# A two-layer kernel on one core: the front's order of work, and the fill of a scatter buffer on another queue

## The chip, the cores and the metric

The kernel runs on 1 core of one Trainium2 chip. The metric is the device time of one execution in microseconds (us), the median of several runs. A core has five engines that work side by side: PE (TensorE, matrix products and transposes), DVE (VectorE), ACT (ScalarE), POOL (GpSimd) and SP (SyncE, which here only issues DMA transfers). They meet through semaphores. SP, ACT and POOL issue transfers, each on its own queue, and all of them are carried by the same 16 DMA engines of the core.

## The reference, cut to what matters

Layer 0 adds to x a selective state-space model (SSM) and a top-1 mixture of 8 experts, both of the layer norm of x. Layer 1 adds attention and a top-4 mixture of 60 experts. There are 2 batches of 1024 tokens, of 256 features each.

```python
xn = _layernorm(x)
x_dbl = einsum('bld,ed->ble', xn, x_proj_w)
dt, B_in, C_in = split(x_dbl, [128, 144])            # 128 step columns, 16 of B, 16 of C
delta = softplus(einsum('blr,dr->bld', dt, dt_proj_w) + dt_proj_b)
dA  = exp(dt_t[..., None] * A[None])                 # per token, feature and one of 16 states
dBx = dt_t[..., None] * B_t[:, None, :] * x_t[..., None]
h = dA * h + dBx
y_t = einsum('bdn,bn->bd', h, C_t) + D_param * x_t
```

## The kernel before

The kernel is written engine by engine; each engine's instructions run in the order written, and that order is set by hand. What the change touches is the front (the first 90 us) and the state loop behind it.

**The front.** `ln(0)` on DVE makes the normalised tokens `xn` in 4 groups of 512 tokens. PE turns each group (L1894), ACT copies it to `xnT` (L1809), PE multiplies it with the step columns (L1904, copied by ACT to `dtT`, L1813) and with the B, C and router columns (L1910, copied by DVE to `bcT`, L1687). `dt_piece(p)` (L1914) projects the step sizes in four pieces: batch p // 2, feature half p % 2. For each piece ACT takes the absolute value, the positive part, an exponential and four squares (L1821 to L1827), and DVE combines them in five steps to `delta` (L1705, L1707); the buffers of a piece are those of `decay`, `state` and `hc`, used in turn by even and odd pieces (L207). PE turns `bcT` (L1926), and DVE copies the B columns `b_col` (L1691) and routes the tokens to the 8 experts (`route_dve`, L420, with a short part on PE, `route_pe`, L477); its `slots_ready` releases 16 indirect DMAs on POOL (`route_pool`, L489), which scatter the tokens to `sorted0`. Before, the routing came on DVE ahead of all four softplus pieces. `delta_rows(b)` (L1932) turns delta back on PE, and DVE multiplies it with `xn` to `dxT` (L1711).

**The fill.** The scatter buffer of layer 1, `sorted1` (124 tiles of 128 rows of 256 numbers, 15.5 MB), has to be zero before it is scattered into. ACT issues this fill behind the softplus pieces, ahead of the state loop: 15 transfers of 1 MB and one of 0.5 MB from a tile of zeros, 128 partitions of 8 KB each (`zero_fill`, L506). Its semaphore `zeroed` is waited for by DVE (L1766) and ACT (L1854) ahead of layer 1.

**The state loop.** 32 iterations `it`, 16 states for each of two batches, and in each two feature halves c. ACT scales `dxT` to `dbxT` (L1842) and makes `decay` (L1848), PE turns `dbxT` into PSUM (`spread`, L1948, its matmuls L1956), DVE scans (L1723), POOL multiplies the scanned state with the C row `crow[:, q]` (L1602, `hc`), and PE sums the products (`gather_sum`, L1959, its matmuls L1962). q is the parity of the iteration. SP brings the C row of each iteration, one DRAM row of 4 KB spread to all 128 partitions (512 KB, L1528); it waits until POOL has finished with that buffer's last row, that is `hc` of iteration it - 2 (`s_hc`, 2 it - 2). The C rows are stored to DRAM first, from 16 partitions (L1521), and they go on SP's queue. Behind the last of them stand, on the same queue, the expert table's store and load (`route_sp`, L501 and L503), a wait for the sums of the state loop, and the expert weights of layer 0 (L536).

Of the kernel before, what the change touches and what calls it, by code (L numbers as in the profile page):

```python
# [65 lines left out]
def build(nc, x_in, a_log, d_param, xproj, dtproj, dt_bias, w13_0, w2_0,  # L66
          router1, w13_1, w2_1, shared13, shared2, wqk, wv_pairs, wo_h, gate_logit, rope, out):
    ctx = ExitStack()
    with ctx:  # L69
# [210 lines left out]
        R1 = Route(TILES1, sorted1, result1, etab1, w13_1, w2_1, TILES1, E1)  # L280
        route_buffers(R1, 1, E1, K1, lambda n, sh, dt=F32: route_early[n] if n in route_early else sbo(n, sh, dt), E1 + 1,
# [1231 lines left out]
        def _(sp):  # L1513
# [117 lines left out]
        def _(v):  # L1631
# [53 lines left out]
            for q in range(NG):  # L1685
                v.wait_ge(s_xb, q + 1)
                v.tensor_copy(bcT[:, q * 512:(q + 1) * 512], ps[0:BCR, 6 + q % 2, :]).then_inc(s_bcc, 1)  # L1687

            v.wait_ge(R0.logits_ready, 1)
# [6 lines left out]

            v.tensor_tensor(R0.weight[:, :, 0], R0.top[:, :, 1], R0.top[:, :, 0], ALU.subtract).then_inc(s_w0, 1)
            for p in range(BATCH * DC):
                b, c = p // DC, p % DC
                cols = slice(b * SEQ, (b + 1) * SEQ)  # L1700
                ex, pos, quads = softplus_buffers(p)
                for k in range(4):
                    v.wait_ge(s_spa, 5 * p + 2 + k)
                    w(v, s_sp, 4 * p + k)
                    v.scalar_tensor_tensor(quads[k], quads[k], FLOORS[k], quads[k - 1] if k else ex, ALU.add, ALU.mult).then_inc(s_sp, 1)  # L1705
                v.wait_ge(s_sp, 4 * p + 4)
                v.scalar_tensor_tensor(delta[:, c, cols], quads[3], LEAD, pos, ALU.mult, ALU.add).then_inc(s_delta, 1)  # L1707
                if c == DC - 1:
                    for n in range(b * (TB // 2), (b + 1) * (TB // 2)):
                        v.wait_ge(s_dlT, n + 1)  # L1710
                        v.tensor_tensor(dxT[:, 2 * n:2 * n + 2, :], ps[:, 6 + n % 2, :].rearrange("p (a d) -> p a d", a=2),  # L1711
                                        xn[:, 2 * n:2 * n + 2, :], ALU.mult).then_inc(s_dxT, 1)
# [81 lines left out]
        def _(act):  # L1794
# [10 lines left out]
            for q in range(NG + 1):  # L1805
                if q < NG:
                    act.wait_ge(s_xnT_ps, q + 1)
                    for c in range(DC):
                        last = act.copy(xnT[:, c, q * 512:(q + 1) * 512], ps[:, (q % 2) * 2 + c, :])  # L1809
                    last.then_inc(s_xnT, 1)  # L1810
                if q:
                    act.wait_ge(s_xd, q)
                    act.copy(dtT[:, (q - 1) * 512:q * 512], ps[:, 4 + (q - 1) % 2, :]).then_inc(s_xdc, 1)  # L1813
            act.wait_ge(s_const, N_CONST + 4)
            for p in range(BATCH * DC):
# [12 lines left out]
            zero_fill(act, R1)  # L1828
# [5 lines left out]
            def terms(b, j):  # L1834
                for q in range(2):
# [8 lines left out]
                    if isinstance(it, int) and it == 0:  # L1844
                        act.wait_ge(s_delta, BATCH * DC)
# [39 lines left out]
        def _(pe):  # L1885
            pe.wait_ge(s_const, N_CONST)
            for q in range(NG + 1):
                if q < NG:
                    pe.wait_ge(s_xn, q + 1)
                    if q >= 2:  # L1890
                        pe.wait_ge(s_xnT, q - 1)
                    for c in range(DC):
                        for i in range(GT):
                            last = pe.transpose(ps[:, (q % 2) * 2 + c, i * P:(i + 1) * P], xn[:, q * GT + i, c * P:(c + 1) * P], ident[:])  # L1894
                    last.then_inc(s_xnT_ps, 1)
                if q:
                    g = q - 1
                    if g == 0:
                        pe.wait_ge(s_par, 80)
                    pe.wait_ge(s_xnT, g + 1)  # L1900
                    if g >= 2:
                        pe.wait_ge(s_xdc, g - 1)
                    for c in range(DC):
                        last = pe.matmul(ps[:, 4 + g % 2, :], xpw[:, c, 0:RANK], xnT[:, c, g * 512:(g + 1) * 512],  # L1904
                                         start=c == 0, stop=c == DC - 1)
                    last.then_inc(s_xd, 1)
                    if g >= 2:
                        pe.wait_ge(s_bcc, g - 1)
                    for c in range(DC):
                        last = pe.matmul(ps[0:BCR, 6 + g % 2, :], xpw[:, c, RANK:XD], xnT[:, c, g * 512:(g + 1) * 512],  # L1910
                                         start=c == 0, stop=c == DC - 1)
                    last.then_inc(s_xb, 1)
# [8 lines left out]
            pe.wait_ge(s_xdc, NG)  # L1921
            for p in range(2):
                dt_piece(p)
            pe.wait_ge(s_bcc, NG)
            for i in range(NT):
                last = pe.transpose(ps[:, 4 + i // 8, (i % 8) * BCR:(i % 8 + 1) * BCR], bcT[:, i * P:(i + 1) * P], ident[0:BCR, 0:BCR])  # L1926
            last.then_inc(R0.logits_ready, 1)
            route_pe(pe, R0)
            for p in range(2, BATCH * DC):
                dt_piece(p)  # L1930

            def delta_rows(b):  # L1932
                pe.wait_ge(s_delta, DC * (b + 1))
                for k in range(TB // 2):
# [156 lines left out]
```

## Time and profile before

| | us |
|---|---|
| median of 3 runs | 1824.44 |
| lowest and highest | 1822.86, 1836.78 |
| the profiled execution's own time | 1827.84 |
| its span | 1826.1 |
| granted TensorE clock, mean, as a share of full speed | 0.976 |

The profile is of one execution, whose own time is 3.4 us above the median. Its span is the time from the first to the last instruction that it shows. Over the span PE is busy for 93%, DVE for 65%, ACT for 56% and POOL for 43%. Busy shares are means over stages with different limits, so the front and the state loop are read for themselves, from the instructions in order of time.

### The profile page before, as it was taken

What the parts mean: (1) busy time and instruction counts of PE and PEld (TensorE: products, weight loads), DVE (VectorE), ACT (ScalarE), POOL (GpSimd) and SP (SyncE); (2) the same over time, 40 slices, a digit from 0 to 9 for tenths busy, and PEclk for the clock granted to TensorE, in tenths of its full rate; (3) what the DMA queues carried; (4) which work ended last, traced back from release to release, by engine and by line L of the source; (5) the groups of instructions that cost most, each with busy time, mean ns of one, the idle gap of its engine ahead of it and who ended that gap; (6) DMA issues with size and microseconds to landing.
All of it is one profiled execution on the core that took longest, in us unless ns stands there. A gap on an engine that the chain in (4) does not pass through costs nothing. (4 is left out here: it accounts for less than half of the span.)

```text
span 1826.1 us, 33417 instructions
## 1 busy us (share of the span) xinstructions
PE 1696.7 (93%) x9234; PEld 1360.4 (74%) x9234; DVE 1194.3 (65%) x2422; ACT 1018.6 (56%) x2287; POOL 778.9 (43%) x789
## 2 busy tenths in 40 slices
PE   6399999489999999999999999999998999999997
PEld 2256556378888888888888888888885777666775
DVE  4799973597887766766767676667662344333476
ACT  4599943267665656665666566666652444434322
POOL 1489861453234544434443444344431342211463
PEclk9699999799999999999999999999999999999999
DMA  4653238500000100000000000001006999999433
GB/s 148 262 221 110 97 116 273 180 12 1 15 9 7 41 13 21 21 6 26 14 11 20 20 20 20 6 26 47 18 30 218 322 325 313 313 302 304 138 95 91
DMA packets 100395, 193.29 MB, mean 106 GB/s; under 512 B 15460, under 2 KB 59748, under 8 KB 97748
## 3 DMA queue, kind: packets, MB, share of 16 engines
q1 hardware_dynamic: 58836, 108.76, 19.1%
q0 software_dynamic: 17152, 47.67, 8.1%
q10 hardware_dynamic: 24336, 35.98, 5.9%
q8 instruction: 35, 0.57, 0.1%
q14 instruction: 36, 0.29, 0.1%
HBM read 140.84 MB, written 51.51 MB: 105 GB/s over the span
## 5 line engine op out<-in xcount | busy, mean ns | idle before, releaser
L1435 POOL TENSOR_TENSOR sw<-sw,rope_t 64x512 f32<-64x512 f32 x128 | 166.1, 1297 | 520.7 <-ACT sw L1048 495.1
L1077 ACT ACTIVATE pb<-ps,negmax 128x128 f32<-128x128 f32 (+7 forms) x256 | 190.8, 745 | 151.2 <-DVE negmax L1288 148.1
L963 PEld LDWEIGHTS ps<-pt,v 128*128 128x128 f32 x1280 | 242.1, 190 | 42.1 <-DVE xr L1316 4.0
L963 PE MATMUL ps<-pt,v 128*128 128x256 f32 (+1 forms) x1280 | 270.7, 358 | 2.8 <-DVE xr L1316 2.6
L561 POOL DMA_DIRECT2D w2r<-in_w x148 | 77.2, 522 | 320.1 <-PE ps L610 278.4
L644 DVE SCALAR_TENSOR_TENSOR ga<-th,ps 128x176 f32<-128x176 f32 x148 | 49.9, 337 | 230.0 <-ACT th L625 230.0
L1288 DVE TENSOR_REDUCE negmax<-ps 128x1 f32<-128x128 f32 (+7 forms) x256 | 193.9, 758 | 8.8
L1064 ACT COPY pt<-ps 128x512 f32<-128x512 f32 (+3 forms) x384 | 171.5, 484 | 38.7 <-PE ps L953 35.6
L1438 POOL TENSOR_TENSOR t<-t,sw 64x512 f32<-64x512 f32 x128 | 167.8, 1311 | 19.2 <-POOL sw L1435 12.8
L593 PE MATMUL ps<-w13r,xt 128*128 128x352 f32 x496 | 169.4, 464 | 0.0
L953 PE MATMUL ps<-ident,pb 128*128 128x128 f32 x1152 | 167.5, 272 | 0.0
L1602 POOL TENSOR_TENSOR hc<-state,crow 128x1024 f32<-128x1024 f32 x64 | 151.2, 2377 | 37.0 <-DVE state L1723 30.6
L610 PE MATMUL ps<-w2r,ht 88*128 88x256 f32 x592 | 154.0, 383 | 5.5 <-DMA w2r<-in_w 3.7
L1723 DVE TENSOR_TENSOR_SCAN state<-decay,ps 128x1024 f32<-128x1024 f32 x64 | 144.8, 2278 | 10.8 <-PE ps L1956 8.8
L883 PE MATMUL ps<-qkr 128*128 128x512 f32 (+3 forms) x384 | 151.1, 394 | 0.7 <-DVE qkl L1276 0.7
L1300 DVE TENSOR_TENSOR t<-ps,rope_t 128x512 f32<-128x512 f32 x124 | 85.6, 690 | 93.7 <-ACT sw L1048 93.6
L1047 ACT COPY sw<-ps 32x512 f32<-32x512 f32 x128 | 74.0, 578 | 115.9 <-PE ps L885 115.2
L953 PEld LDWEIGHTS ps<-ident,pb 128*128 128x128 f32 x1152 | 133.7, 141 | 0.1
L885 PE MATMUL ps<-qkl,qkr 128*128 128x512 f32 (+3 forms) x384 | 133.0, 346 | 0.0
L884 PE MATMUL ps<-qkr,qkl 128*128 128x512 f32 (+3 forms) x384 | 132.7, 346 | 0.0
L630 ACT COPY yy<-ps 128x256 f32<-128x256 f32 x148 | 55.1, 373 | 125.2 <-PE ps L610 121.0
L1962 PE MATMUL ps<-hc,ident 128*128 128x512 f32 x256 | 120.0, 594 | 1.7 <-DVE delta L1745 1.1
(245 smaller groups left out, 4004.6 us busy)
## 6 DMA issues: line engine op xcount, KB each, us to landing
w13r<-in_w SPq DMA_DIRECT2D x124, 352.0 KB, 5.5
w2r<-in_w POOLq DMA_DIRECT2D x148, 176.0 KB, 5.8
result<-yy ACTq DMA_DIRECT2D x148, 128.0 KB, 4.9
crow<-c_rows SPq DMA_DIRECT2D x32, 512.0 KB, 3.5
t<-sorted SPq DMA_DIRECT2D x124, 128.0 KB, 5.1
sorted<-zeros ACTq DMA_DIRECT2D x15, 1024.0 KB, 16.9
hc<-in_w SPq DMA_DIRECT2D x24, 352.0 KB, 5.1
wraw<-in_wqk SPq DMA_DIRECT2D x16, 256.0 KB
```

What stands on the lines that cost most here:

```text
L593: last = pe.matmul(ps[:, GU_BANK[b % 2], 0:2 * INNER], r.xt[:, b % 2, c * P:(c + 1) * P], r.w13[:, b, c], start=c == 0, stop=c == DC - 1)
L610: last = pe.matmul(ps[:, DN_BANK[b % 2], 0:D], r.ht[:, b % 2, c], r.w2[:, b, c], start=c == 0, stop=c == 1)
L883: pe.matmul(out_ap, a_r, b_r, start=start, stop=False)
L953: last = pe.transpose(ps[:, 4 + ci % 2, (j - j0) * P:(j - j0 + 1) * P], pb[:, qt % 2, j * P:(j + 1) * P], ident[:])
L963: last = pe.matmul(ps[:, 6, c0:2 * P], v[:, j, hd], pt[g % 2][:, j, c0:2 * P], start=j == 0, stop=j == 2 * g + 1)
L1064: act.copy(pt[g % 2][:, j0:j1, cols], ps[:, 4 + ci % 2, 0:(j1 - j0) * P].rearrange("p (j q) -> p j q", q=P)).then_inc(s_pl, 1)
L1077: act.activation(pb[:, qt % 2, 0:cols], ps[:, bank:bank + 2, :].rearrange("p a n -> p (a n)")[:, 0:cols], ACT.Exp, bias=negmax[:, par, qn: ...
L1288: dve.tensor_reduce(negmax[:, par, qn:qn + 1], ps[:, bank:bank + 2, :].rearrange("p a n -> p (a n)")[:, 0:cols], AX.X, ALU.max, negate=Tru ...
L1435: g.tensor_tensor(sw[64:128, p % 2, :], sw[64:128, p % 2, :], rope_t[64:128, 1, (p // 2) * 512:(p // 2 + 1) * 512], ALU.mult).then_inc(s_t ...
L1438: g.tensor_tensor(t1[64:128, p % 2, :], t1[64:128, p % 2, :], sw[64:128, p % 2, :], ALU.add).then_inc(s_rot, 1)
L1602: g.tensor_tensor(hc[:, q, c], state[:, q, c], crow[:, q], ALU.mult).then_inc(s_hc, 1)
L1723: v.tensor_tensor_scan(state[:, q, c], decay[:, q, c], ps[:, 4 + 2 * c:6 + 2 * c, :].rearrange("p a t -> p (a t)"), 0.0, ALU.mult, ALU.add ...
```

## The change

The fill leaves ACT's queue. SP issues it in 32 pieces, one behind each C row: 496 rows of `sorted1`, which are 124 partitions of the tile of zeros with 4 KB each (4 rows to a partition). `zeroed` counts 32 transfers in place of 16.

In the front, the loops over the four token groups are taken apart. PE projects the step sizes of the first batch (pieces 0 and 1) right after the four groups are turned, ahead of the B and C columns of all groups and of the step columns of groups 2 and 3. DVE takes softplus pieces 0, 1 and 2, the B and C rows between them, and `input_rows(0)`, ahead of the routing; piece 3 comes after the routing. PE turns the first batch's delta ahead of `bcT`. ACT takes piece 0 ahead of the step columns of groups 2 and 3. The first `decay` waits for three deltas, the second for the fourth.

```diff
+        R1.zero_dmas = BATCH * STATES
 ...
+            FILL_ROWS = R1.routed * P // (BATCH * STATES)
+
             def c_row(b, j):
                 for q in range(2):
                     it = 2 * j + q
                     w(sp, s_hc, 2 * it - 2)
                     sp.dma_start(crow[:, q, :], c_rows[bass.ds(it - b * STATES, 1), b * SEQ:(b + 1) * SEQ]
                                  .to_broadcast([P, SEQ])).then_inc(s_crow[q], 16)
+                    sp.dma_start(R1.slots[bass.ds(it * FILL_ROWS, FILL_ROWS), :].rearrange("(p a) d -> p (a d)", a=4),
+                                 zeros[0:FILL_ROWS // 4, 0:4 * D]).then_inc(R1.zeroed, 16)
 ...
+            softplus(0)
+            take_bc_rows(0)
+            take_bc_rows(1)
+            softplus(1)
+            take_bc_rows(2)
+            take_bc_rows(3)
+            softplus(2)
+            input_rows(0)
             v.wait_ge(R0.logits_ready, 1)
 ...
             route_dve(v, R0)
-
             v.tensor_tensor(R0.weight[:, :, 0], R0.top[:, :, 1], R0.top[:, :, 0], ALU.subtract).then_inc(s_w0, 1)
-            for p in range(BATCH * DC):
 ...
+            softplus(3)
+            input_rows(1)
 ...
-            zero_fill(act, R1)
+            take_group(0)
+            take_group(1)
+            take_dt_rows(0)
+            take_group(2)
+            take_dt_rows(1)
+            take_group(3)
+            act.wait_ge(s_const, N_CONST + 4)
+            softplus(0)
+            take_dt_rows(2)
+            take_dt_rows(3)
+            for p in range(1, BATCH * DC):
+                softplus(p)
 ...
-                    if isinstance(it, int) and it == 0:
-                        act.wait_ge(s_delta, BATCH * DC)
+                    if isinstance(it, int) and it < 2:
+                        act.wait_ge(s_delta, 3 + it)
 ...
             def dt_piece(p):
                 b, c = p // DC, p % DC
+                pe.wait_ge(s_xdc, 2 * b + 2)
                 if p >= 2:
                     pe.wait_ge(s_dpc, 2 * p - 2)
+                else:
+                    pe.wait_ge(s_xnT, p + 3)
 ...
+            turn_group(0)
+            turn_group(1)
+            pe.wait_ge(s_par, 80)
+            dt_rows(0)
+            turn_group(2)
+            dt_rows(1)
+            turn_group(3)
+            for p in range(2):
+                dt_piece(p)
+            bc_rows(0)
+            bc_rows(1)
+            dt_rows(2)
+            dt_rows(3)
+            for p in range(2, BATCH * DC):
+                dt_piece(p)
+            bc_rows(2)
+            bc_rows(3)
+            pe.wait_ge(s_bcc, NG)
+            delta_rows(0)
+            for i in range(NT):
+                last = pe.transpose(ps[:, 4 + i // 8, (i % 8) * BCR:(i % 8 + 1) * BCR], bcT[:, i * P:(i + 1) * P], ident[0:BCR, 0:BCR])
+            last.then_inc(R0.logits_ready, 1)
+            pe.wait_ge(s_dxT, TB // 2)
+            route_pe(pe, R0)
             pe.wait_ge(R0.slots_ready, 1)
-            delta_rows(0)
             delta_rows(1)
```

## Rows read from the trace of the kernel before

**Rows 1.** Timeline, ACT and its queue around the fill: start, us, engine, instruction [idle before].
```profile
67.96 17.22 ACTq L512 DMA_DIRECT2D sorted<-zeros  x12
85.22 0.23 ACT L1830 ACTIVATE weight<-weight 128x16 f32<-128x16 f32 x1 [16.16 <-issue]
```
**Rows 2.** Timeline, POOL and PE from the routing to the first sums.
```profile
46.99 0.17 DVE L470 CAST slot<-slotf 128x16 uint32<-128x16 f32 x1
70.38 1.02 POOL L495 DMA_INDIRECT sorted<-xn,slot  x1 [0.30 <-issue]
...
88.39 3.65 PE L1956 MATMUL ps<-ident,dbxT 128*128 128x128 f32 x16 [6.26 <-ACT dbxT L1842]
92.87 9.52 POOL L1602 TENSOR_TENSOR hc<-state,crow 128x1024 f32<-128x1024 f32 x4 [21.47 <-DVE state L1723]
98.97 1.88 PE L1962 MATMUL ps<-hc,ident 128*128 128x512 f32 x4
```
**Rows 3.** Waits between 60 and 130 us: who waited for whom, us, times, longest.
```profile
POOL hc L1602 <- DMA crow<-c_rows: 5.3, 1, 5.3
```
**Rows 4.** Timeline, two sums of the same half, one iteration apart, late in the loop.
```profile
233.82 1.88 PE L1962 MATMUL ps<-hc,ident 128*128 128x512 f32 x4
...
239.01 1.88 PE L1962 MATMUL ps<-hc,ident 128*128 128x512 f32 x4
```
**Rows 5.** Timeline of the front: pieces of work whose durations the new order reuses.
```profile
20.97 1.88 PE L1904 MATMUL ps<-xnT,xpw 128*128 128x512 f32 x4
...
35.05 1.11 ACT L1821 ACTIVATE decay<-ps,dtb 128x1024 f32<-128x1024 f32 x1 [3.23 <-PE ps L1919]
37.82 0.49 DVE L1691 COPY b_col<-ps 128x128 f32<-128x128 f32 x2 [4.06 <-PE ps L1926]
42.31 1.09 ACT L1821 ACTIVATE decay<-ps,dtb 128x1024 f32<-128x1024 f32 x1
...
65.36 1.22 DVE L1705 SCALAR_TENSOR_TENSOR state<-state,decay 128x1024 f32<-128x1024 f32 x1
70.60 1.22 DVE L1707 SCALAR_TENSOR_TENSOR delta<-hc,decay 128x1024 f32<-128x1024 f32 x1
```
**Rows 6.** DMA queue, 38 to 44 us, two C rows: packets, MB, share of 16 engines.
```profile
DMA packets 288, 1.05 MB, mean 175 GB/s; under 512 B 32, under 2 KB 32, under 8 KB 288
q1 hardware_dynamic: 288, 1.05, 47.5%
```
**Rows 7.** The same from 34 to 36 us, then 34.3 to 35.3: the C rows' store, 16 partitions.
```profile
DMA packets 33, 0.15 MB, mean 74 GB/s; under 512 B 16, under 2 KB 16, under 8 KB 16
...
q1 hardware_dynamic: 16, 0.13, 101.3%
```
**Rows 8.** The same from 255 to 261 us: the expert table's load into one partition.
```profile
q1 hardware_dynamic: 2, 0.00, 0.0%
```
**Rows 9.** The same from 65.4 to 65.9 us: the fill's first packets, 128 partitions, 8 KB each.
```profile
q10 hardware_dynamic: 16, 0.13, 64.8%
```
**Rows 10.** Page, DMA issues: KB each, median us to landing.
```profile
crow<-c_rows SPq DMA_DIRECT2D x32, 512.0 KB, 3.5
```
**Rows 11.** Issues of one line, first and last start; then DMA view, 249 to 257 us.
```profile
L1528 SPq DMA_DIRECT2D crow<-c_rows x32: 332/333/433, 38.4 to 249.5; - x32
...
crow<-c_rows SPq DMA_DIRECT2D x1, 512.0 KB, 3.7
etab<-ecoli SPq DMA_DIRECT2D x1, 0.5 KB, 7.7
```
**Rows 12.** Timeline, SP's queue and the engines at the end of the loop.
```profile
250.05 0.33 SPq L501 DMA_DIRECT2D etab<-ecoli  x1
254.56 8.75 PE L1962 MATMUL ps<-hc,ident 128*128 128x512 f32 x20
257.72 0.29 SPq L503 DMA_DIRECT2D etabrow<-etab  x1
261.17 0.61 POOL L561 DMA_DIRECT2D w2r<-in_w  x1 [1.52 <-issue]
264.34 3.69 SPq L536 DMA_DIRECT2D hc<-in_w  x4
```

More of the change, by code:

```diff
@@ L1683, in _, with take_bc_rows, softplus, input_rows @@
             v.wait_ge(s_const, N_CONST)
-            for q in range(NG):
+            def take_bc_rows(q):
                 v.wait_ge(s_xb, q + 1)
                 v.tensor_copy(bcT[:, q * 512:(q + 1) * 512], ps[0:BCR, 6 + q % 2, :]).then_inc(s_bcc, 1)
+            def softplus(p):
+                b, c = p // DC, p % DC
+                ex, pos, quads = softplus_buffers(p)
+                for k in range(4):
+                    v.wait_ge(s_spa, 5 * p + 2 + k)
+                    w(v, s_sp, 4 * p + k)
+                    v.scalar_tensor_tensor(quads[k], quads[k], FLOORS[k], quads[k - 1] if k else ex, ALU.add, ALU.mult).then_inc(s_sp, 1)
+                v.wait_ge(s_sp, 4 * p + 4)
+                v.scalar_tensor_tensor(delta[:, c, b * SEQ:(b + 1) * SEQ], quads[3], LEAD, pos, ALU.mult, ALU.add).then_inc(s_delta, 1)
+            def input_rows(b):
+                for n in range(b * (TB // 2), (b + 1) * (TB // 2)):
+                    v.wait_ge(s_dlT, n + 1)
+                    v.tensor_tensor(dxT[:, 2 * n:2 * n + 2, :], ps[:, 6 + n % 2, :].rearrange("p (a d) -> p a d", a=2),
+                                    xn[:, 2 * n:2 * n + 2, :], ALU.mult).then_inc(s_dxT, 1)
+            softplus(0)
[6 more added lines that the diff above has]
+            input_rows(0)
             v.wait_ge(R0.logits_ready, 1)
@@ L1697, in _ @@
             v.tensor_tensor(R0.weight[:, :, 0], R0.top[:, :, 1], R0.top[:, :, 0], ALU.subtract).then_inc(s_w0, 1)
-            for p in range(BATCH * DC):
[L1699 to L1712, printed above, removed]
+            softplus(3)
+            input_rows(1)
             v.wait_ge(s_w0, 2)
@@ L1803, in _, with take_group, take_dt_rows, softplus @@
             act.mul(aneg[:], alog[:], -1.0).then_inc(s_aneg, 1)
[L1805 to L1815, printed above, removed]
+            def take_group(q):
+                act.wait_ge(s_xnT_ps, q + 1)
+                for c in range(DC):
+                    last = act.copy(xnT[:, c, q * 512:(q + 1) * 512], ps[:, (q % 2) * 2 + c, :])
+                last.then_inc(s_xnT, 1)
+            def take_dt_rows(g):
+                act.wait_ge(s_xd, g + 1)
+                act.copy(dtT[:, g * 512:(g + 1) * 512], ps[:, 4 + g % 2, :]).then_inc(s_xdc, 1)
+            def softplus(p):
                 c = p % DC
@@ L1886, in _ @@
             pe.wait_ge(s_const, N_CONST)
[L1887 to L1912, printed above, removed]
@@ new lines, in turn_group, with dt_rows @@
+            def turn_group(q):
+                pe.wait_ge(s_xn, q + 1)
+                if q >= 2:
+                    pe.wait_ge(s_xnT, q - 1)
+                for c in range(DC):
+                    for i in range(GT):
+                        last = pe.transpose(ps[:, (q % 2) * 2 + c, i * P:(i + 1) * P], xn[:, q * GT + i, c * P:(c + 1) * P], ident[:])
+                last.then_inc(s_xnT_ps, 1)
+            def dt_rows(g):
+                pe.wait_ge(s_xnT, g + 1)
+                if g >= 2:
+                    pe.wait_ge(s_xdc, g - 1)
+                for c in range(DC):
+                    last = pe.matmul(ps[:, 4 + g % 2, :], xpw[:, c, 0:RANK], xnT[:, c, g * 512:(g + 1) * 512],
+                                     start=c == 0, stop=c == DC - 1)
+                last.then_inc(s_xd, 1)
@@ L1914, in dt_piece, with bc_rows @@
+            def bc_rows(g):
+                pe.wait_ge(s_xnT, g + 1)
+                if g >= 2:
+                    pe.wait_ge(s_bcc, g - 1)
+                for c in range(DC):
+                    last = pe.matmul(ps[0:BCR, 6 + g % 2, :], xpw[:, c, RANK:XD], xnT[:, c, g * 512:(g + 1) * 512],
+                                     start=c == 0, stop=c == DC - 1)
+                last.then_inc(s_xb, 1)
             def dt_piece(p):
                 b, c = p // DC, p % DC
+                pe.wait_ge(s_xdc, 2 * b + 2)
@@ L1920, in dt_piece @@
                               start=True, stop=True).then_inc(s_dp, 1)
[L1921 to L1930, printed above, removed]
             def delta_rows(b):
```

## The prediction

> **What bounds the kernel now.** I read the timeline first, from 20 us to the layer-0 experts, then the waits, then the DMA view of single transfers. From 98.97 us on, PE makes one sum after the other, and two sums of the same half stand 5.19 us apart [rows 2, 4]: PE sets the state loop's pace. POOL needs about 2 x 2.38 = 4.76 us of it (9.52 us for four products) [rows 2]. So the front is worth what it moves the first sum at 98.97, as long as nothing slower than 5.19 enters the loop. What holds the front is ACT: it issues 12 of the 16 fill transfers from 67.96 to 85.2, idle for 16.16 us, and the first `dbxT` comes behind that [rows 1]; PE spreads at 88.39, POOL's first product starts at 92.87 [rows 2]. The C row behind the fill then costs POOL 5.3 us once [rows 3]. The loop ends on PE at 254.56 + 8.75 = 263.31, and the experts' weights are issued at 264.34 [rows 12].
>
> **The front in its new order.** PE multiplies a group with the step columns in 1.88 us [rows 5]. Without the B, C columns in between, pieces 0 and 1 can be projected by about 24.3, where the first ACT step of piece 0 stood at 35.05. A piece takes ACT 42.31 - 35.05 = 7.26 us and DVE 70.60 + 1.22 - 65.36 = 6.46 [rows 5]; DVE can begin when the first square is there, 4.2 us into ACT's piece. I get delta 0 at 35.1 and, with the step columns of groups 2 and 3 between (ACT restarts at 34.4, when they are projected), delta 1 at 45.2. Two copies of B, C rows and piece 2 give delta 2 at 53.1; `input_rows(0)` takes 3.6 (half prepared by PE during piece 2): 56.7. PE's wait for all B, C rows (46.6) stands ahead of `delta_rows(0)` and costs nothing, as DVE is in piece 2 until 53.1. PE then turns `bcT`: 57.3. From the B columns to the slots it was 47.16 - 37.82 = 9.34 us [rows 2, 5], so the slots are ready at 66.7 in place of 47.16. Piece 3 ends at 74.0 and `input_rows(1)` at 78.7, where PE's first spread can begin (88.39 before). ACT, free of the fill, has both first `dbxT` and `decay` ready by then. The first scan starts near 80.9.
>
> But the routing is now late, and behind its slots stand POOL's 16 indirect DMAs, which took from 47.16 to 71.40, 24.2 us [rows 2]. They now end at 90.9, ahead of POOL's first product. It starts there, 2 us earlier than 92.87, not 9. Still the first sum gains more: before, ACT's ramp held PE until 98.97; now the sum follows the product at 90.9 + 2.4 = 93.4, with PE spreading in the gaps: 5.5 us. The stalls behind the late C row, some 0.9 us on PE against its pace, go too. **Front: -6.4 us**, and this is what the change gives if the fill costs nothing.
>
> **The fill in the loop.** SP issues it behind each C row; two issues of some 0.35 us per 5.19 are nothing. The question is on how many DMA engines it runs. One small packet is left per engine used: 32 for two 128-partition transfers with 256 others, 16 for the store from 16 partitions with 16 others, one for the load into one partition with one other [rows 6 to 8]. So a transfer is dealt out in equal shares of rows: 16 x 8, 16 x 1, 1 x 1. 124 partitions don't go into 16 equal shares; the largest number of engines up to 16 that they do is 4, with 31 rows each. No transfer before has such a count; the bounds are 1 engine and 16. I take 4.
>
> The price of a row: 8 KB from the tile of zeros took 0.648 x 8 / 16 = 0.324 us [rows 9], so 4 KB 0.162. A second fact is in the store: its packets have the same size and direction, but come from 16 neighbouring partitions, and took 1.013 x 16 / 16 = 1.013 us each, 3.1 times as long [rows 7]. Engines that read near partitions at the same time slow each other. Four engines at 31 rows' distance walk in step; whether they meet no row shows. Bounds: 0.162 us (never) and 0.507 (as in the store). Sixteen readers gave one 8 KB packet per 1.013 / 16 us; if they meet by fours, a meeting place yields one per 0.253 us, and a pair of engines would need 0.506 for 8 KB each, 0.253 for 4 KB. I take the pair, between the ends: it is 1.56 times the free price, the mildest meeting there is. **Fill: 31 x 0.253 = 7.84 us per piece** on the four engines. The C row's own share is 0.475 x 6 / 2 = 1.43 us per engine [rows 6]. Together 9.27 us per iteration, against 5.19.
>
> The Trainium skill's page "SBUF — State Buffer", section "Door 1: The DMA port swizzle", has partitions 32 apart on the same port, at 27.2 GB/s each; 31 apart is the same port for three rows in four. By that a shared row would take 0.301 us, the piece about 8.2 and the sum below about 11 us more. The slow store agrees in kind (129 GB/s from 16 partitions); what four engines do no run here shows. The Trainium skill's page "DMA: Bandwidth & Descriptors", section "Why a DMA increments its semaphore by 16 and not by 1", gives as number of engines the largest divisor up to 16, here 4; with 16 the sum would be the rival below.
>
> Now the chain: four engines serve row, fill, row, fill in order of issue, and POOL cannot start iteration `it` before its row has landed. Row 2 is issued when POOL ends iteration 0 at 95.8, and lands 3.5 us later [rows 10]: 99.3. From there each row follows the last by 9.27: row 31 at 99.3 + 29 x 9.27 = 368.1. POOL is done 4.8 later, but that isn't the end: on SP's queue the table's store stands behind the last fill, 368.1 + 7.84 = 376.0. Before, it was issued at 250.05 and took 7.7, to 257.75; the row issued at 249.5 took 3.7, to 253.2, so 4.5 after it [rows 11, 12]. Then 261.17 - 257.72 = 3.45 for the load, and 264.34 - 263.31 = 1.03 until the first weights [rows 12]. So the weights start at 376.0 + 4.5 + 3.45 + 1.03 = 385.0, where they did at 264.34: **+120.6 us**. The sum behind PE's last products is then hidden, and the front's 6.4 us are inside this (row 2 is issued 2 us earlier). Everything behind moves with it; the `zeroed` waits come over 100 us later still. Against the profiled execution: 1827.8 + 120.6 = 1948.4; it is 3.4 above the median, so **predicted 1945 us**.
>
> **The rivals.**
> (a) *Few engines, meeting nobody.* 31 x 0.162 = 5.02 us, 6.45 per iteration. Row 31 lands at 286.4, the weights start at 286.4 + 5.0 + 9.0 = 300.4: +36, **1860 us**. For it: four readers are far fewer than 16, and far apart. Against: the store's factor of 3.1.
> (b) *The fill is dealt out to all 16 engines after all* (some with 8 rows, some with 7). Then it takes 8 x 0.162 = 1.3 us on each, 2.7 with the row, inside 5.19, and rows land in time: **1818 us**, no slower. This decides as soon as the price of fill and row on the busiest engine is under 5.19 us. For it: every large transfer before runs on all 16 at 25 GB/s each. Against: the equal shares of all three kinds of rows.
> (c) *Few engines that meet as in the store.* 31 x 0.507 = 15.7, 17.1 per iteration: row 31 at 596, +356, **2180 us**. For: the store is the only row with near partitions. Against: its readers stood side by side.
> (d) *The front loses.* If POOL's indirect DMAs start later than 66.7, its first product is late by as much. It would show only under (b), where it decides against a gain from 6.4 us on.
>
> **How the numbers follow.** The likeliest, 4 engines in pairs: 0.51, by itself 1921 to 1966 (a shared row 10% cheaper or dearer than 0.253 us gives +97 or +141 by the same steps). (a) 0.29, (b) with (d) inside it 0.13, (c) 0.07. With (b) and (c) left out 0.80 remain, so the range is **1848 to 1968**, from (a) with packets 7% quicker than in their rows (+23) to the likeliest's upper end. Within 1% is about what a measurement of this kernel can tell from no change. Faster by over 1% needs 18 us, which no case gives; 0.02, taken from the slower ones, are left for it. Within 1%: (b), 0.13. Slower: 0.85.
>
> **What would show each step.** In the DMA view of a stretch of the loop, small packets per iteration: 16 + 4 = 20 for four engines, 32 for sixteen. The distance of two of POOL's products two apart: 9.3 us, or 6.5, 17, or 5.2. POOL's idle time in the loop put down to the C rows' DMA, some 31 waits of 4 to 5 us. The slots cast near 66.9, POOL's first product near 91, PE's first sum near 93.4. The table's store landing over 10 us after the last C row's issue. PE would be busy for 5.2 of 9.3 us; its granted clock there is to be read too, but it costs only if PE becomes slower than the rows. The prediction is wrong if the fill's packets are spread evenly, or if far partitions don't slow each other.

## The result, and the profile after

| | us |
|---|---|
| after, median of 6 runs | 1864.64 (1857.32 to 1870.63) |
| before, median of 6 runs beside them | 1827.68 (1822.86 to 1836.78) |
| ratio | 1.0198, interval 1.0162 to 1.0234 |
| the profiled execution after: own time, span | 1857.32, 1855.6 |

The change makes the kernel 37 us slower, 2.0%. The prediction was 1945 us, 80 us too much; the measured time is that of its rival (a). The profiled execution of after is the quickest of its six, so the traces show 29.5 us of the difference (spans 1855.6 and 1826.1) and leave 7.5 us of the medians' 37 unexplained.

Timeline of after, the end of the routing on DVE, then POOL (start, us, engine, instruction [idle before]):

```profile
65.18 0.17 DVE L471 CAST slot<-slotf 128x16 uint32<-128x16 f32 x1
66.32 2.06 POOL L496 DMA_INDIRECT sorted<-xn,slot  x1 [49.00 <-DVE slot L471]
...
86.57 0.97 POOL L496 DMA_INDIRECT sorted<-xn,slot  x1 [0.31 <-issue]
87.56 11.90 POOL L1607 TENSOR_TENSOR hc<-state,crow 128x1024 f32<-128x1024 f32 x5
94.10 2.68 PE L2004 MATMUL ps<-hc,ident 128*128 128x512 f32 x4
```

These answer [rows 2]: the slots come at 65.2 in place of 47.0, the first product at 87.6 in place of 92.9, the first sum at 94.1 in place of 99.0. The front gains. Then POOL in the loop, its waits from 60 to 300 us (total, times, longest), and the page's DMA issues (KB each, median us to landing):

```profile
152.79 4.69 POOL L1607 TENSOR_TENSOR hc<-state,crow 128x1024 f32<-128x1024 f32 x2 [1.36 <-DMA crow<-c_rows]
158.90 4.68 POOL L1607 TENSOR_TENSOR hc<-state,crow 128x1024 f32<-128x1024 f32 x2 [1.42 <-DMA crow<-c_rows]
...
268.11 4.65 POOL L1607 TENSOR_TENSOR hc<-state,crow 128x1024 f32<-128x1024 f32 x2 [1.38 <-DMA crow<-c_rows]
279.24 4.64 POOL L1607 TENSOR_TENSOR hc<-state,crow 128x1024 f32<-128x1024 f32 x2 [6.48 <-DMA crow<-c_rows]
```
```profile
POOL hc L1607 <- DMA crow<-c_rows: 44.7, 29, 6.5
```
```profile
crow<-c_rows SPq DMA_DIRECT2D x32, 512.0 KB, 7.0
```

The two pairs of products, one pair for each iteration, start 6.1 us apart (6.07 over 27 iterations), where PE's own pace was 5.19 [rows 4]. Where before had one wait of 5.3 us for a C row [rows 3], there are now 29. The DMA view of 206 to 212 us says why. Its second line is the rate in 40 equal slices:

```profile
GB/s 109 109 109 109 109 109 109 109 246 246 164 273 410 410 410 328 382 437 382 191 109 109 109 109 109 109 82 109 82 109 109 109 109 109 109 109 109 109 109 109
DMA packets 272, 1.03 MB, mean 172 GB/s; under 512 B 20, under 2 KB 20, under 8 KB 272
```

There are 20 small packets in an iteration, 16 of the C row and 4 of the fill. For most of the time the rate stands near 109 GB/s, which is four packets to a slice of 0.15 us; now and then there are three. A stretch of 3 us without the slices, 209.3 to 212.3, gives the mean:

```profile
DMA packets 83, 0.32 MB, mean 105 GB/s; under 512 B 6, under 2 KB 6, under 8 KB 83
```

That is four engines at 26.3 each, 0.156 us for a row of 4 KB. The trace's records of single packets agree: on one engine the starts are 0.155 us apart (209.267, 209.422, 209.578, 209.733). An iteration gives each of the four engines 31 such rows of the fill and 8 of the C row, 39 x 0.155 = 6.05 us; the pace measured is 6.07.

At the loop's end, SP's queue, POOL and PE in the timeline, and one of SP's waits from 262 to 292 us:

```profile
266.92 0.36 SPq L1531 DMA_DIRECT2D crow<-c_rows  x1
267.47 0.29 SPq L1533 DMA_DIRECT2D sorted<-zeros  x1
267.97 0.33 SPq L502 DMA_DIRECT2D etab<-ecoli  x1
281.63 6.28 PE L2004 MATMUL ps<-hc,ident 128*128 128x512 f32 x8 [6.26 <-POOL hc L1607]
284.14 0.25 SPq L504 DMA_DIRECT2D etabrow<-etab  x1
288.94 2.57 SPq L537 DMA_DIRECT2D hc<-in_w  x3
```
```profile
SPq L1538 <- PE ps L2004: 3.5, 1, 3.5
```

The weights go out at 288.94, 24.6 us later than in [rows 12]. The last C row takes 12.3 us to land, to 279.2, where the others take 7. POOL's and PE's last work hangs on it: PE's sums end at 281.63 + 6.28 = 287.91, and 1.03 us later the weights go out, the same 1.03 as in [rows 12]. The table's load, issued at 284.14, was done before; SP then waited 3.5 us for PE.

Behind that one more difference stands. Attention, from the first to the last copy of one line of ACT (L1048 before, L1049 after), lasts from 394.8 to 1378.5, 983.7 us; in the trace of before it was 369.6 to 1345.2, 975.6 us. So 24.6 us were there when the weights went out, and attention added 8.1. The way from the weights to attention added 0.6, and what follows attention was 3.8 us shorter, which makes the spans' 29.5. ACT's waits from 400 to 1380 us in after hold two rows that the trace of before lacks:

```profile
ACT pt L1065 <- issue: 8.9, 4, 2.4
ACT qkr L1084 <- issue: 7.2, 4, 1.8
```

### The profile page after: what moved, and what is told of

Same layout as the page of the kernel before. It is cut to its first block and busy times, and to the rows that moved or that the text cites. A ratio compares the mean times of both kernels' runs of the same rounds, so it can differ in the third digit from the quotient of the medians.

```text
span 1855.6 us, 33498 instructions
## 1 busy us (share of the span) xinstructions
PE 1710.2 (92%) x9234; PEld 1366.4 (74%) x9234; DVE 1217.8 (66%) x2422; ACT 1021.6 (55%) x2287; POOL 776.4 (42%) x789
## 5 line engine op out<-in xcount | busy, mean ns | idle before, releaser
L1048 ACT COPY sw<-ps 32x512 f32<-32x512 f32 x128 | 74.0, 578 | 113.0 <-PE ps L886 111.7
L2004 PE MATMUL ps<-hc,ident 128*128 128x512 f32 x256 | 125.7, 617 | 9.3 <-POOL hc L1607 6.3
```

## The experiments

Each kernel ran beside before on the same chip. The level differs from group to group, and not with the chip alone: the median of before was 1817.6 us beside e1 to e4 and 1831.8 beside e7, e8, e13 and e14, on one and the same chip; it was 1816.6 beside e6 and e10 to e12, and 1831.7 beside e15 to e18. In the traces most of this stands behind attention: from its end to the end of the span it is 464 to 472 us beside the lower medians and 475 to 484 in all others, whatever the edit (481 in before, 477 in after). So only ratios, and times up to attention's end, go across groups.

### First set: front or fill, four engines or sixteen

e1 keeps the change, but takes each piece from 128 partitions:

```diff
-R1.slots[...].rearrange("(p a) d -> p (a d)", a=4), zeros[0:124, 0:4 * D]
+R1.slots[...] as 128 x 992 numbers, zeros[0:128, 0:992]
```

> The changed kernel with one edit: each of the 32 fill pieces (still 496 rows, still on SP's queue behind the C row) is taken from 128 partitions with 3968 bytes each in place of 124 with 4096. Theory (few engines): the piece then runs on 16 engines, some 1.3 us on each; with the row's 1.4 that is under PE's 5.19 us per iteration, so the products of the same half stand 5.19 us apart in place of 6.06, 32 small packets per iteration in place of 20, and the time is about 6 us under before, ratio 0.996 to 0.998. Rival (shared queue): any fill between the rows on one queue delays them, whatever its spread; then the pace stays above 5.5 us and the time at least 10 us above before. Rival (new front): the front costs by itself; then the pace is 5.19 but the time is above before.

e2 keeps the new front and leaves the fill on ACT; e3 keeps before's front and moves the fill as the change does; e4 is e3 with pieces from 128 partitions.

```diff
-sp.dma_start(R1.slots[...], zeros[...])      # e2: behind each C row
+zero_fill(act, R1)                           # e2: behind softplus
```

> The new front alone: the order of work of the changed kernel, the fill as before (16 transfers, 128 partitions, on ACT's queue, behind the fourth softplus piece). Theory (few engines): pace 5.19 us, no loss in the loop. ACT has its gap from 55 to 66 us for the fill, but issuing took some 20 us before, so its first dbxT comes near 75 in place of 66, and row 2, issued near 92, still meets the end of the fill. First product 87 to 89, a gain of 2 to 6 us over before, ratio 0.996 to 0.999. Rival (new front): slower than before by itself, ratio over 1.002.

> The fill alone: the front's order as before, the fill in 32 pieces of 124 partitions on SP's queue. Theory (few engines): pace 6.06 us per iteration as in the changed kernel, ratio 1.016 to 1.023, like the whole change. With the fill off ACT, PE's first spread can begin near 83, POOL's first product near 87.5, the same as with the new front. Rival (new front carries the loss): ratio under 1.01.

> The front's order as before and the fill in 32 pieces of 128 partitions (3968 bytes each) on SP's queue. Theory (few engines): pace 5.19, first product near 87.5, first sum near 93.5, about 5 us under before, ratio 0.996 to 0.998, the same as the new front with such pieces; the new order in the front then is worth within 2 us of nothing, since POOL's indirect DMAs, late behind the late routing, take back what it brings. Rival (the front pays): the version with both edits is over 4 us faster than this one.

| | ratio, interval | first product | first sum | weights issued | attention |
|---|---|---|---|---|---|
| e1 | 0.9993, 0.9971 to 1.0016 | 88.8 | 91.2 | 257.7 | 981.5 |
| e2 | 0.9962, 0.9937 to 0.9987 | 88.7 | 91.1 | 259.6 | 975.1 |
| e3 | 1.0173, 1.0141 to 1.0205 | 88.7 | 94.9 | 291.5 | 981.7 |
| e4 | 1.0011, 0.9986 to 1.0035 | 88.8 | 94.9 | 259.0 | 981.4 |

The fill on four engines is what makes the change slower: 124 partitions become 128 and 1.020 becomes 0.999. In e1 POOL waits for a C row once, 0.2 us, small packets are 32 to an iteration, and the pace is PE's 5.19. The weights go out 6.6 us earlier than before. The front alone gives 4.7 (e2), and the fill on 16 engines behind the C rows with the old front gives 5.3 (e4), so the two gains overlap: on top of e4 the new front brings 1.3 us, and the ratios of e1 and e4 are not apart. e1 and e4 lose part of it again behind the loop: their attention takes 981 us, e2's 975. It is 981 to 984 in every kernel here whose fill has left ACT with nothing in its place, with the loop slow or fast. ACT's waits in e1 from 380 to 1360 us, and one occurrence in its timeline:

```profile
ACT pt L1065 <- issue: 9.1, 4, 2.4
ACT qkr L1084 <- issue: 6.5, 4, 1.6
```
```profile
758.91 0.27 ACT L1065 COPY pt<-ps 128x128 f32<-128x128 f32 x1 [2.35 <-issue]
760.79 0.62 ACT L1084 CAST qkr<-t 128x512 fp32r<-128x512 f32 x1 [1.61 <-issue]
```

ACT stands for nothing that the profile shows. But the queue q14, which carries instructions, has more to do there: 38 loads in e1, 39 in after, 20 in before, 17 in e2. The fill's 16 issues took up 1024 bytes of ACT's program (compiled, it has 107072 bytes in before and e2 and 106048 in after, e1, e3 and e4), and without them all that follows lies 1024 bytes earlier.

### Second set: code placement, an earlier routing, the table's store, two engines

```diff
 for p in range(1, BATCH * DC):
     softplus(p)
+for _ in range(32):
+    act.wait_ge(s_const, 1)       # met long ago; ACT's program is 107072 bytes again
```

> The changed kernel with two edits: pieces of the fill from all 128 partitions (as in e1), and 32 semaphore waits that are met already, written on ACT where the fill's 16 issues stood. They take up 1024 bytes of ACT's program, as much as the fill did, and nothing else moves. Theory that code placement makes attention longer: ACT's waits put down to issue at L1065 and L1084 between 380 and 1360 us (9.1 and 6.5 us in e1) go, the code loads there fall from 38 to about 20, and attention takes 975 us as in e2 and before, where it took 981.5 in e1. Span about 1809.5, ratio 0.995 to 0.996. Theory that the fill on SP's queue itself costs the 6 us (more DMA work late, or the zeroed semaphore that comes later): everything as in e1, attention 981.5, ratio 0.999.

e11: ratio 0.9963, interval 0.9943 to 0.9983; attention from 365.7 to 1340.8, 975.1 us. Both rows of waits for issue are gone, and the instruction loads from 380 to 1360 us:

```profile
q14 instruction: 17, 0.14, 0.0%
```

PE shows where the time was: busy 117.03 of the 120 us from 760 to 880 in e1, 118.69 in e11 (windows of both kernels; over 400 to 1360 us it is 937.2 and 943.8, 6.6 us more):

```profile
760.00:880.00 120.00, 117.03 (x712) 103.56 (x710) 82.16 (x167) 76.03 (x173) 47.93 (x48) 1.00 0.05 18
```
```profile
760.00:880.00 120.00, 118.69 (x720) 105.09 (x718) 81.79 (x167) 75.47 (x172) 49.21 (x49) 1.00 0.05 17
```

The placement of ACT's code is shown as the cause, since the waits are all that differs between e1 and e11. That the loads replace code which the loop has pushed out is argued from their count.

e12 is e11 with the routing right behind softplus piece 1 on DVE, ahead of `delta_rows(0)` on PE:

```diff
             softplus(1)
             take_bc_rows(2)
             take_bc_rows(3)
-            softplus(2)
-            input_rows(0)
             (b_col, route_dve)
+            softplus(2)
+            input_rows(0)
             softplus(3)
```

> e11 with the routing moved ahead on DVE and PE: DVE takes the B columns and the routing right behind softplus piece 1, ahead of piece 2 and input_rows(0), and PE turns delta of the first batch behind the routing. Theory that POOL's 16 indirect DMAs (21.2 us in after's trace) bound the first product in the new front: slots ready near 55.5 in place of 65.2, the DMAs end near 77, and the first product then waits for the first scan, near 81 to 83; first sum near 85, 6 us ahead of e1 (91.2). If the state loop's pace of 5.19 holds, the weights are issued near 252 and the ratio is 0.992 to 0.993, 3 to 6 us under e11. Rival: something else holds the first product (the C row's landing, or ACT's first decay): it stays at 87 to 89 and the ratio is that of e11.

e12: ratio 0.9921, interval 0.9892 to 0.9949, the fastest here: 12 us under before on its chip (1804.5 and 1816.6). POOL in its timeline:

```profile
58.27 2.05 POOL L496 DMA_INDIRECT sorted<-xn,slot  x1 [40.68 <-DVE slot L471]
...
79.20 0.97 POOL L496 DMA_INDIRECT sorted<-xn,slot  x1 [0.30 <-issue]
83.46 24.17 POOL L1607 TENSOR_TENSOR hc<-state,crow 128x1024 f32<-128x1024 f32 x10 [3.29 <-DVE state L1737]
```

Now the scan ends the wait and no longer POOL's own DMAs. The weights go out at 253.7, 3.5 us before e11's 257.2. The slots came 1.7 us later than expected (57.2), and the first sum at 89.0, not 85: it gained 2.2 us on e1's 91.2, less than expected.

e10 puts the table's store behind the landing of the last C rows:

```diff
             state_pairs(sp, c_row)
+            sp.wait_ge(s_crow[1], 16 * BATCH * STATES // 2)
             route_sp(sp, R0)
```

> The changed kernel with one more wait: SP issues the expert table's store only when the last two C rows have landed. In after's trace the last row took 12.3 us to land where the others took about 7, and the DMA engines stood nearly idle for 5 us right after the table store's 128 packets of 4 bytes. Theory that the tiny packets hold up the row and the piece of fill behind it: the last row lands about 7 us after its issue, near 274 in place of 279.2, POOL's last product ends near 279; the table store, issued near 274, lands later, so that the weights are issued near 288 to 290 as before; ratio against before 1.018 to 1.021. Rival, that the end of the row stream itself (no further row, POOL idle) makes it slow: it still lands 12 us after its issue, near 279, the store is issued then, the weights near 300, ratio 1.025 to 1.027.

e10: ratio 1.0173, interval 1.0138 to 1.0207. Timeline:

```profile
267.83 0.36 SPq L1531 DMA_DIRECT2D crow<-c_rows  x1
274.88 0.33 SPq L502 DMA_DIRECT2D etab<-ecoli  x1
275.10 4.64 POOL L1608 TENSOR_TENSOR hc<-state,crow 128x1024 f32<-128x1024 f32 x2 [1.40 <-DMA crow<-c_rows]
285.90 0.25 SPq L504 DMA_DIRECT2D etabrow<-etab  x1
288.97 2.98 SPq L537 DMA_DIRECT2D hc<-in_w  x3
```

The last row lands in 7 us again, so the table's store, 128 packets of 4 bytes, held it for 5 us in after. But the weights go out at 288.97, as in after, and here another wait ends last: PE's sums end at 281.8, and SP waits for the table, whose store now lands 11.0 us after its issue at 274.88, and whose load takes 3.1 more.

```profile
SPq L535 <- DMA etabrow<-etab: 1.8, 1, 1.8
```

So two chains end close together. In after it was the late row, by way of POOL and PE; with the row on time it is the table, which started 6.9 us later. In after the table alone would have let the weights go at about 284.14 + 3.07 = 287.2 (an estimate from these rows), so the row's delay cost after about 1.7 us, and not 5.

e6 takes the pieces from 62 partitions of 8 KB.

```diff
-zeros[0:124, 0:4 * D]
+zeros[0:62, 0:8 * D]
```

> The changed kernel with the fill's pieces taken from 62 partitions of 8 KB each, so that by equal shares 2 engines carry 31 packets of 8 KB. Theory that the number of engines times the packet's own time sets the pace: a packet of 8 KB takes 0.30 us (27.3 GB/s), a piece 9.3 us, with the row's share of 1.4 us 10.7 us per iteration; 18 small packets per iteration; C rows make POOL wait about 5 to 6 us in each; the last row's landing near 420 and the weights near 430, +165 us; ratio 1.085 to 1.095. Rival, that a stream from few engines is bound by something common to them (the engines' sum, 109 GB/s in after): 2 engines reach the same 109 GB/s, the pace stays 6.1 us and the ratio 1.02.

e6: ratio 1.0927, interval 1.0888 to 1.0966; 10.74 us per iteration, 18 small packets, 53 GB/s between the rows (206 to 210 us), 0.309 us for each packet of 8 KB. Half the engines, twice the time: the pace is set by the work of one engine.

### Third set: who meets whom

The step that failed said that the four engines meet. In these kernels they stand still: each reads one partition, 31 times 4 KB, and the choice of the partitions is all that differs.

```diff
-zeros[0:124, 0:4 * D]
+zeros[0:4,     0:4 * D] x 31        # e13
+zeros[0:128:32, 0:4 * D] x 31       # e14: 0, 32, 64, 96
+zeros[1:95:31, 0:4 * D] x 31        # e15: 1, 32, 63, 94
+zeros[0:16:4,  0:4 * D] x 31        # e16: 0, 4, 8, 12
+zeros[0:128:64, 0:4 * D] x 62       # e17: 0, 64; two engines
```

> The changed kernel with the fill's piece read from 4 partitions side by side (0 to 3), each read 31 times, 4 KB a time; the same 31 packets for each of 4 engines, the same places written. Theory of the prediction, that engines which read near partitions at the same time slow each other as in the store from 16 partitions: a packet costs at least 0.253 us (16 readers shared one 8 KB packet per 0.063 us, and four meeting all the time give 4 KB per 0.127 to 0.25 us each), pace 9.3 us per iteration, ratio about 1.07. Rival, that a reader's neighbours don't matter and a packet costs what it costs in after (0.150 us at 27.3 GB/s for each engine): pace 6.06 us, 20 small packets per iteration, ratio 1.017 to 1.020.

> [...] By that rule a packet of 4 KB costs 4 x 0.150 = 0.60 us, the piece 18.6 us, and the pace is 20 us per iteration (ratio about 1.23). Rival, that four engines read at their own 27.3 GB/s wherever the rows lie: pace 6.06 us, ratio 1.017 to 1.020, as e13 and after.

> As e13 and e14, but from partitions 1, 32, 63 and 94, 31 apart as the four shares of the changed kernel, each read 31 times: the engines stand still instead of walking. Theory that groups share a path (by the Trainium skill's page SBUF - State Buffer, section Door 1, partitions 1 and 32 share a port, 63 and 94 do not) and that the changed kernel escapes because its engines walk out of step: the pair at 1 and 32 pays 0.30 us a row as in e14, pace 10 to 10.5 us per iteration, ratio 1.07 to 1.09. Rival, that 31 apart shares nothing: pace 6.06 us, ratio 1.017 to 1.020, as after.

> The same from partitions 0, 4, 8 and 12, near each other but in four groups of four neighbours. Theory that only a fixed group of partitions shares a path: each engine has its own, 0.150 us a row, pace 6.06 us, ratio 1.017 to 1.020. Rival, that nearness slows (the store from 16 partitions and e13 as two cases of it): a row costs between 0.25 and 0.61 us, pace 9 to 20 us, ratio 1.07 to 1.25.

> The fill's piece from partitions 0 and 64, each read 62 times: two engines. Theory that 0 and 64 don't share a path, and in e14 0 and 32 did: 62 x 0.150 + 1.43 = 10.7 us per iteration as in e6, 18 small packets, ratio 1.09. Rival, that in e14 0 and 64 were the pair that shared: 62 x 0.30 + 1.4 = 20 us, ratio 1.24.

Two pairs of POOL's products in e13, e14, e15 and e16, from their timelines:

```profile
161.07 4.65 POOL L1607 TENSOR_TENSOR hc<-state,crow 128x1024 f32<-128x1024 f32 x2 [15.76 <-DMA crow<-c_rows]
181.42 4.65 POOL L1607 TENSOR_TENSOR hc<-state,crow 128x1024 f32<-128x1024 f32 x2 [15.69 <-DMA crow<-c_rows]
```
```profile
147.71 4.65 POOL L1607 TENSOR_TENSOR hc<-state,crow 128x1024 f32<-128x1024 f32 x2 [5.90 <-DMA crow<-c_rows]
157.97 4.66 POOL L1607 TENSOR_TENSOR hc<-state,crow 128x1024 f32<-128x1024 f32 x2 [5.61 <-DMA crow<-c_rows]
```
```profile
163.33 4.66 POOL L1607 TENSOR_TENSOR hc<-state,crow 128x1024 f32<-128x1024 f32 x2 [4.57 <-DMA crow<-c_rows]
172.77 4.68 POOL L1607 TENSOR_TENSOR hc<-state,crow 128x1024 f32<-128x1024 f32 x2 [4.79 <-DMA crow<-c_rows]
```
```profile
152.37 4.68 POOL L1607 TENSOR_TENSOR hc<-state,crow 128x1024 f32<-128x1024 f32 x2 [1.36 <-DMA crow<-c_rows]
158.44 4.68 POOL L1607 TENSOR_TENSOR hc<-state,crow 128x1024 f32<-128x1024 f32 x2 [1.40 <-DMA crow<-c_rows]
```

| partitions read | pace, us | us per 4 KB row | ratio, interval |
|---|---|---|---|
| after: 31 apart, walking | 6.07 | 0.156 | 1.0198, 1.0162 to 1.0234 |
| e16: 0, 4, 8, 12 | 6.07 | 0.156 | 1.0147, 1.0108 to 1.0187 |
| e17: 0, 64 (62 rows each) | 10.88 | 0.155 | 1.0926, 1.0889 to 1.0963 |
| e15: 1, 32, 63, 94 | 9.48 | 0.266 | 1.0689, 1.0655 to 1.0723 |
| e14: 0, 32, 64, 96 | 10.33 | 0.293 | 1.0802, 1.0730 to 1.0874 |
| e13: 0, 1, 2, 3 | 20.36 | 0.617 | 1.2490, 1.2454 to 1.2527 |

The price is (pace - 1.24) / 31 (e17: / 62), where 1.24 is the C row's 8 x 0.155. The packet records of 170 to 230 us show it directly, in steps: 0.159 us alone (after, e16, e17), 0.28 to 0.34 with one other reader (542 packets in e14, 298 in e15), 0.60 to 0.63 with three (320 packets in e13). In after 2247 of its 2501 packets of 4 KB took 0.159, and 34 took 0.28 to 0.34: its engines hardly ever meet. In e15 the pair's price is a mean; the two are not always at the fill together, but 62 rows in 9.48 us are 26.8 GB/s, so their common path is never idle for long. Nearness doesn't decide, since 4 apart is free; the group does. Four partitions side by side share one path of 27 GB/s (4 x 4096 / 0.617 = 26.6), 0 and 32 share one, 0 and 64 don't. The Trainium skill's page "SBUF — State Buffer", section "Door 1: The DMA port swizzle", has this map: four neighbours and the four that lie 32 above them on one port of 27.2 GB/s, those 64 above on the other port of the cluster. All five kernels agree. For e14 0.60 us a row was expected, as if all four lay on one port; by the page's table 0 and 32 are on one port and 64 and 96 on another, so two readers to a port and not four, and that is what came.

And e15 settles why the changed kernel is free of it. Its four shares are 31 apart as well, but in e15, where they can't move, a row costs 0.266 us, and in the changed kernel, where they walk, 0.156. The small packets show that the walkers are out of step. Each engine leaves one where it ends its fill and another 1.25 us later, behind its C row. In after (DMA view of 210.1 to 210.9, of 210.9 to 211.3, of 211.3 to 211.6 and of 211.6 to 211.8):

```profile
DMA packets 22, 0.09 MB, mean 108 GB/s; under 512 B 1, under 2 KB 1, under 8 KB 22
```
```profile
DMA packets 10, 0.04 MB, mean 92 GB/s; under 512 B 1, under 2 KB 1, under 8 KB 10
```
```profile
DMA packets 9, 0.03 MB, mean 96 GB/s; under 512 B 2, under 2 KB 2, under 8 KB 9
```
```profile
DMA packets 8, 0.03 MB, mean 143 GB/s; under 512 B 1, under 2 KB 1, under 8 KB 8
```

By the packet records four engines end their pieces at 210.21, 211.01, 211.44 and 211.68, and their C rows at 211.46, 212.26, 212.69 and 212.92 (of the two small packets of the third view one is of each kind). So they are up to 1.5 us apart, nine rows. Two engines on the same group of four partitions need to be only some rows out of step to be in different groups, and as SP's queue is never empty, a lag once gained stays. What made the lag stays open: the loop's first pieces have slow packets of the fill and of the C row alike, and no run tells them apart.

e8 reads 16 partitions side by side, four times 7936 bytes each, and e7 64 partitions of 7936 bytes:

```diff
-zeros[0:124, 0:4 * D]
+zeros[0:16, 0:1984] x 4              # e8
+zeros[0:64, 0:1984]                  # e7
```

> The changed kernel with the fill's piece read from 16 partitions (0 to 15), each four times, 7936 bytes a time: 16 engines with 4 packets each, from 16 neighbouring partitions as in the C rows' store, whose packets took 1.013 us in before's trace. Theory that 16 neighbouring readers slow each other: a packet takes about 0.98 us, a piece 3.9 us, with the row's 1.4 us 5.4 us per iteration, just over PE's 5.19: C rows make POOL wait a little in each iteration, ratio 1.000 to 1.006. Rival, that the store is slow for another reason (a cold start, its data): a packet takes 0.30 us, a piece 1.2 us, no waits for rows, pace 5.19, ratio 0.999 as e1.

> The changed kernel with the fill's piece read from 64 partitions of 7936 bytes: 16 engines by equal shares, 4 packets each. Theory of equal shares and free engines: a packet takes 0.30 us, 32 small packets per iteration, no waits for rows, pace 5.19, ratio 0.999 as e1. Rival, that half the partitions give half the bandwidth (readers 4 partitions apart meet): a packet takes 0.6 us, a piece 2.4 us, with the row 3.8 us per iteration, still under 5.19: seen in the fill's landing (about 7 us instead of e1's 5.2) and not in the time.

e8: ratio 1.0028, interval 1.0009 to 1.0047. POOL's waits from 60 us on, and the page's issues:

```profile
POOL hc L1607 <- DMA crow<-c_rows: 12.2, 19, 0.9
```
```profile
sorted<-zeros SPq DMA_DIRECT2D x32, 496.0 KB, 7.8
```

The pace is 5.35 over the nine iterations up to 180 us and 5.27 over the eight from 214. The store's slowness [rows 7] is reproduced by its partitions alone, for 16 neighbours are four groups of four: of e8's 696 packets of the fill from 170 to 230 us, 197 took 1.19 to 1.24 us, four times the 0.30 that 196 others took. e7: ratio 1.0010, interval 0.9990 to 1.0030, fill landing in 5.0 us. The time is that of the first theory, and so is the price for the most part: 532 of 707 packets of the fill took 0.30 us and 89 took 0.58 to 0.62, the rival's price, with a mean of 0.36.

### Fourth set: the changed kernel with its code moved back

e18 is the changed kernel with e11's 32 waits and nothing else.

> The changed kernel with nothing but the 32 met waits on ACT of e11. Theory that the loss has two parts, 24.6 us until the weights' issue (the loop's pace) and 6 to 8 in attention (code loads on ACT): the weights are issued near 289 as in after, attention takes 975 us in place of 983.7, 17 to 20 code loads between 380 and 1360 us, span about 1849, ratio 1.013 to 1.015. Rival, that attention is longer because of something in the long loop before it: 983 us, ratio 1.018.

e18: ratio 1.0144, interval 1.0118 to 1.0170. The weights go out at 290.4, attention takes 975.7 us (396.5 to 1372.2), and 20 instruction loads stand in 380 to 1360 us. So the loss of the change has two parts: 24.6 us of the loop, net of the front's gain, and 8 us of code placement. The second stands on the traces of attention and not on e18's ratio: e16, at the same pace and without the waits, has 1.0147.

## Why the prediction was wrong, by its own steps

**Number of engines: right.** 4 from 124 partitions: 20 small packets, 105 GB/s, and e6's two engines for 62. Rival (b) was false for the change, and e1 shows what it would have been: 0.9993.

**The price of a row: the step that failed.** It took 0.253 us, from a pair that meets; 0.156 was measured, just below the free price of 0.162 from [rows 9]. The pace became 6.07 in place of 9.27, the last row landed at 279.2 (about 274 without the store's delay) in place of 368.1, and +120.6 us at the weights became +24.6. The C row's own share was 1.25 us and not 1.43. The reasoning had a true half: readers that share a group do slow each other, and a pair costs 0.266 to 0.293 (e15, e14). It lacked that engines which walk need not stay together. "Walk in step" was assumed; the store could not show it, as each of its engines has one packet only [rows 7].

**Rival (a)** gave 1860 us and 1864.6 came, but partly by luck. Its loop was 6.45 us per iteration and +36 at the weights; the trace has 6.07 and +24.6. What fills the gap no step had: attention's 8 us, and the 7.5 us by which the medians differ more than the traces. A small slip in the sums: a row 10% dearer gives +144 us and not +141, which changes nothing here.

**The chain at the loop's end: near in its sum, wrong in its path.** From a last row at 274 it gives 4.8 for the piece + 4.5 + 3.45 + 1.03 = 287.8; measured 288.9. That is luck. The prediction had the sums behind PE's last products hidden behind the table; in after they ended last. The store held the row for 5 us, to 279.2; then POOL's products and PE's sums ran until 287.91, and 1.03 us later the weights went out. The table's store took 16.2 us in after and 11.0 in e10 from its issue to the load's, where it took 7.7 in [rows 12].

**The front: right in its order, and in its size partly by luck.** Slots at 65.4 (predicted 66.7). From there to the end of POOL's 16 indirect DMAs it was 22.2 us and not 24.2, since only the first was long (2.06 us; before, three were: 2.06, 2.00, 1.70), so the first product stood at 87.6 in place of 90.9. The first sum came at 94.1, against 93.4. It followed the product by 6.5 us in after and not by 2.4; in e1, e2, e10 and e11, with the same front, it followed by 2.4. "-6.4 us if the fill costs nothing" is e1's -6.6 at the weights' issue. As time of the whole kernel e2 gives 0.9962 and e11 0.9963, 6 to 7 us. Rival (d) didn't come. The granted clock, which was to be read, is 1.00 in the loop of after from 100 to 250 us but for 0.96 from 180 to 220 (1.00 throughout in before), and POOL's products keep their distance of 6.1 us there.

**What was missing.** Removing 16 instructions from ACT was taken to be free once the queue was clear. It moved ACT's attention code, and that cost 6 to 8 us, as much as the front gained.

## What to carry to other kernels

The number of rows of a transfer decides how many DMA engines carry it: give a large transfer 128 partitions (64 and 16 ran on 16 engines as well, but some or most of their readers met, e7 and e8), and count the small packets in one stretch of the DMA view to see what it got. Before an engine's order is changed, ask what stands behind its longest chain of short steps, as here POOL's indirect DMAs behind the slots; routing right behind the second softplus piece was worth another 3.5 us at the weights (3.7 by the medians of e11 and e12, whose intervals overlap). When a change moves time in a stage that it doesn't touch, look for waits put down to issue and for the count of instruction loads there; waits that are met already, written where instructions were removed, test it in one run.

## What the runs showed of the hardware beyond what was expected

- Readers of one group of partitions share 27 GB/s: 0.156 us for a 4 KB row alone, 0.293 for two, 0.617 for four (e16, e14, e13). The same distance of 31 partitions costs 0.266 when standing still and nothing when walking (e15, after).
- The number of engines at work did not change a fill row's price: in e1, on 16 engines, each of 1408 packets of 3968 bytes from 170 to 230 us took 0.154 us, and in after, on four, a packet of 4096 took 0.159. What got slower beside the fill on 16 engines were the C row's packets, 0.270 us in the mean in e1 and 0.186 in before.
- 1024 bytes less in ACT's program doubled the instruction loads in a loop behind (38 in place of 17) and stopped ACT for 15.6 us, of which 6 reached the time (e1 and e11).
- A store of 128 packets of 4 bytes held a C row that was issued before it for 5 us (12.3 us to landing in after, 7 in e10).
